# Loading the edge rows as 96 partitions and a rest, and making the first norm in two parts, in a graph network kernel

## The chip, the cores and the metric

The kernel runs on one core of one Trainium2 chip. The metric is the device time of one execution in microseconds (us, lower is better), as the median of three runs. The engines are named as in the profile: PE (TensorE, with PEld for its weight loads), DVE (VectorE), ACT (ScalarE), POOL (GpSimd) and SP (SyncE, which here only issues DMAs); PEq, ACTq and SPq are their instruction queues.

## The reference, cut to what matters

Four graph layers run one after the other on 6250 nodes of 128 features and 206250 edges sorted by destination. Each begins with a layer norm and a ReLU and adds its result to `x`. Only the first is touched here:

```python
h = relu(layernorm(x))                                        # the first norm
h_all = einsum('nd,rdf->nrf', h, weight)                      # 8 relations
gate_all = einsum('nd,rdo->nro', h, gate_weight)[..., 0]
msg = h_all[src, rel_type] * norm * sigmoid(gate_all[src, rel_type])[:, None]
out = relu(segment_sum(msg, dst, num_segments=6250))
```

## The kernel before

The nodes are padded to 6272, which is 49 tiles (`NT`) of 128 partitions. Before the edges of the first layer are walked, a setup block does two things side by side. All line numbers are those of the kernel before.

**The table.** The block makes `h`, the normed and rectified `x`, in 7 pieces (`PIECES`) of 7 tiles, and then a table in HBM (`table0`) that holds `sigmoid(gate) * h @ weight` for each node and relation, 512 KB for a tile of nodes. For tile t the work goes around four engines. PE turns `h[:, t, :]` over (L548), ACT copies the result out of PSUM (L492), PE multiplies it by the gate weights (L552) and by the eight relation weights (L558, called P(t) in what follows), ACT makes the sigmoid (L499), DVE scales four relations (L694, `gates`) and ACT the other four (L507), and SP stores the tile (L434, `store`). The staging buffer `out` has three places, so `gates(t)` and the ACT half of it wait until the store of tile t-3 has landed. P(t) waits for `gates(t-2)`, since PSUM has two places.

**The index work.** Beside it DVE checks whether the edges are sorted, finds the span of each chunk of 512 edges, and makes keys for pairs of nodes. It reads `dst_rows` (101 partitions, one for each round of 2048 edges) and `later` (the same list shifted by 256 edges). SP writes `rows_t` to HBM in four DMAs of 832 KB (L427), and POOL gathers from this table and from another (L649, L655).

The order on each engine's queue is written out by hand. SP issues its DMAs in program order, and the stores of the table stand behind L413, L417, L419, L422 and the four of L427:

```python
sp.dma_start(dst_rows, ...)                    # L413: 101 partitions
sp.dma_start(later[0:full, :], ...)            # L417: full = 100 partitions
sp.dma_start(later[full:full + 1, ...], ...)   # L419
sp.dma_start(next_first[0:ROUNDS - 1, :], ...) # L422: 100 elements
sp.wait_ge(s_rows_t, 7)
for k in range(MPT): sp.dma_start(flat_table[...], rows_t[...])  # L427, 4 times
store(0, 11)
```

On DVE the norm (`norm_vector`, L137) runs through the whole of `x` in each step before the next: the mean over all 49 tiles, seven subtractions, seven sums of squares, one variance, and after ACT's square root the seven scalings. Only behind the fifth and the seventh of these do the first `gates` come. ACT (`norm_scalar`, L165) alternates Square and ReLU over the pieces, then does one Sqrt, and only then begins with the tiles. Between calls of `gates`, DVE's index work is spread over tiles 4 to 45 (L709 to L839). PE has some of it too: `last_rows` (L571) after tiles 12 and 16, and `flip` (L584) after every second tile from 23 on.

The block ends with a barrier, and the loop over edges begins after it.

Of the kernel before, what the change touches and what calls it, by code (L numbers as in the profile page):

```python
# [18 lines left out]
NB = 4  # L19
ROUNDS = -(-E // (CH * NB))  # L20
# [9 lines left out]
EPS = 1e-5  # L30
# [22 lines left out]
PIECES = 7  # L53
PT = NT // PIECES
# [4 lines left out]
LIMIT = 256  # L59


def bass_gnn(nc, A):

    root = ExitStack()
    with root:
# [68 lines left out]
        def piece(k):  # L134
            return slice(k * PT, (k + 1) * PT)
# [131 lines left out]
        FLIPS = -(-PCOLS // 2)  # L267
        s_marks_in = root.enter_context(nc.semaphore("pair_marks_in"))
# [29 lines left out]
        with ExitStack() as l0:  # L298
# [17 lines left out]
            with ExitStack() as st:  # L316
# [81 lines left out]
                def _(sp):  # L398
# [3 lines left out]
                    for k in range(MPT):  # L402
# [10 lines left out]
                    sp.dma_start(dst_rows, A["dst_rows"].rearrange("(p k) e -> p (k e)", k=NB)).then_inc(s_rows, 16)  # L413
# [3 lines left out]
                    sp.dma_start(later[0:full, :], flat_dst[LIMIT:LIMIT + full * span]  # L417
                                 .rearrange("(p e) -> p e", e=span)).then_inc(s_later, 16)
# [17 lines left out]
                    store(0, 11)  # L436
                    sp.wait_ge(s_mark_t, 1)
                    sp.dma_start(flat_pairs[0:PSPAN].rearrange("(k p) -> k p", p=P), mark_t[:, :]).then_inc(s_mark_out, 16)
                    store(11, 13)
# [7 lines left out]
                    store(13, 20)  # L447
# [3 lines left out]
                    store(20, 22)  # L451
# [5 lines left out]
                    store(22, 38)  # L457
                    sp.wait_ge(s_gout, 2)
                    sp.dma_start(A["groups"].rearrange("(r a) b -> r a b", a=2), gout[:, :, :]).then_inc(s_g_out, 16)
                    store(38, 40)  # L460
# [3 lines left out]
                    store(40, NT)  # L464
# [5 lines left out]
                @block.scalar  # L470
                def _(act):
                    act.dma_start(rel, A["rel_cols"]).then_inc(s_rel, 16)
                    act.dma_start(x[:, :, :], A["x"].rearrange("(t p) d -> p t d", p=P)).then_inc(s_x, 16)
                    act.dma_start(w0[:, :].rearrange("p (r d) -> p r d", r=R), A["w0"].rearrange("r k d -> k r d")).then_inc(s_w, 16)
                    with nc.allow_non_contiguous_dma(reason="1024 gate weights, once"):
                        act.dma_start(g0[:, :], A["g0"].rearrange("r k a -> k (r a)")).then_inc(s_w, 16)
                    act.dma_start(weight0[:, :], A["weight_cols"]).then_inc(s_w, 16)
                    for b in range(0, BLOCKS, 2):
                        n = min(2, BLOCKS - b)
                        act.wait_ge(s_turned, 2 * (b + n))  # L480
                        nc.scalar.activation(rows_t[:, b:b + n, :, :].rearrange("p b e w -> p b w e"),
                                             pS[:, b // 2 % 2, 0:n * 2 * P].rearrange("p (b w e) -> p b w e", b=n, w=2),
                                             ACT.Copy).then_inc(s_rows_t, 1)
# [38 lines left out]
                    step(11, 22)  # L522
                    for m in range(FLIPS):
                        step(22 + 2 * m, 24 + 2 * m)
                        flip(m)
                    step(22 + 2 * FLIPS, NT + 2)
                    act.wait_ge(s_key, FLIPS)
                    act.wait_ge(s_x, 16)
                    act.wait_ge(s_w, 48)

                @block.tensor
                def _(pe):
# [55 lines left out]
                    step(0, 8)  # L588
# [3 lines left out]
                    step(8, 11)  # L592
                    pe.wait_ge(s_mark, 1)
                    nc.tensor.transpose(pS[0:PCOLS, 0, 0:P], mark[:, :], ident[:, :]).then_inc(s_mark_turned, 1)
                    step(11, 13)
# [5 lines left out]
                    step(13, 17)  # L601
# [3 lines left out]
                    step(17, 22)  # L605
                    for m in range(FLIPS):
                        step(22 + 2 * m, 24 + 2 * m)
                        flip(m)
                    step(22 + 2 * FLIPS, NT + 1)

# [50 lines left out]
                def _(dve):  # L661
# [36 lines left out]
                    def behind_norm(k):  # L698
                        if k == 4:
                            gates(0, 1)  # L700
                        if k == 6:
                            gates(1, 4)
                    dve.wait_ge(s_x, 16)
                    norm_vector(dve, norm0, h, between=behind_norm)

                    dve.wait_ge(s_rows, 16)
# [3 lines left out]
                    gates(4, 5)  # L710
                    dve.wait_ge(s_fall, 1)
                    nc.vector.tensor_reduce(fall[0:ROUNDS, 0:1], falls, AXX, ALU.max).then_inc(s_fall, 1)
                    gates(5, 7)
# [7 lines left out]
                    gates(7, 9)  # L721
                    dve.wait_ge(s_below, 2)
                    nc.vector.tensor_reduce(in_round[:, :], behind, AXX, ALU.add).then_inc(s_below, 1)
                    gates(9, 10)
# [19 lines left out]
                    gates(10, 12)  # L744

                    dve.wait_ge(s_later, 32)
                    nc.vector.memset(over[:, :], 0.0).then_inc(s_repeat, 1)
                    nc.vector.tensor_tensor(repeats, dst_rows, later, ALU.is_ge).then_inc(s_repeat, 1)
                    gates(12, 14)
                    dve.wait_ge(s_repeat, 2)  # L750
                    nc.vector.tensor_reduce(over[0:ROUNDS, :], repeats, AXX, ALU.max).then_inc(s_repeat, 1)
                    gates(14, 15)
# [6 lines left out]
                    cover(0)  # L759
                    cover(1)  # L760
                    gates(15, 16)
                    nc.vector.tensor_reduce(low[:, :, 0], by_chunk, AXX, ALU.min).then_inc(s_low, 1)
                    gates(16, 18)
                    cover(2)
                    cover(3)
                    gates(18, 19)
# [4 lines left out]
                    gates(19, 21)  # L771
# [16 lines left out]
                    gates(21, 23)  # L788
# [5 lines left out]
                    gates(23, 25)  # L794
                    keys(1)
                    gates(25, 27)
# [5 lines left out]
                    gates(27, 29)  # L802
                    keys(2)
                    gates(29, 31)
# [3 lines left out]
                    gates(31, 33)  # L808
                    keys(3)
                    gates(33, 35)  # L810
# [23 lines left out]
                    gates(35, 37)  # L834
                    keys(4)
                    gates(37, 41)
                    keys(5)
                    gates(41, 45)
                    keys(6)  # L839
                    gates(45, NT)  # L840
# [1347 lines left out]
```

## Time and profile before

| | |
|---|---|
| median of three runs | 6237.64 us (6236.5 to 6240.86) |
| the profiled execution | 6241.27 us, span 6239.5 us |
| setup block in the span | 0 to about 191 us |
| busy PE / DVE / ACT / POOL | 75% / 42% / 24% / 50% |
| DMA | 817.56 MB, mean 131 GB/s |

The setup block is some 3% of the span. It can be read from a timeline alone, since each instruction of it runs once or 49 times; the pages' averages over the whole span say little about it.

### The profile page before, as it was taken

The numbers are of one execution on the slowest core, as the hardware profiler recorded it, in microseconds if no ns is written. First come the engines' busy times: TensorE is split into PE (matmuls) and PEld (weight loads), VectorE is DVE, ScalarE is ACT, GpSimd is POOL, SyncE is SP. The second block draws the span as 40 slices with busy tenths as digits, with TensorE's granted clock in tenths as the row PEclk, the third lists the DMA queues.
The fourth block names the chain that finished last, engine by engine and source line by source line (L and its number), as shares of the span: only waits on it lengthen the run. The fifth ranks groups of instructions, "written<-read, shape, count | busy, mean of one in ns | idle before, by whom it ended". The sixth has DMA issues, their size and how long they took to land. (4 is left out here: it accounts for less than half of the span.)

```text
span 6239.5 us, 90775 instructions
## 1 busy us (share of the span) xinstructions
PE 4667.4 (75%) x25783; PEld 3126.0 (50%) x25784; DVE 2634.3 (42%) x6089; ACT 1472.9 (24%) x2786; POOL 3137.0 (50%) x3319
## 2 busy tenths in 40 slices
PE   5555555555555548888888888888899799999998
PEld 3444444444444435555555555555444444444444
DVE  6666666666666554444444444444312300000000
ACT  4211111111111123333333333333211211111000
POOL 3577777777777727777777777776000000000000
PEclk9555555555555568888888888888799899999999
DMA  6333333322333324444344434443345365555554
GB/s 218 110 94 94 94 94 94 92 87 84 93 94 94 105 80 125 132 133 133 125 131 133 133 123 133 133 133 96 136 159 162 99 200 191 187 193 190 192 193 150
DMA packets 337345, 817.56 MB, mean 131 GB/s; under 512 B 126590, under 2 KB 147633, under 8 KB 321059
## 3 DMA queue, kind: packets, MB, share of 16 engines
q1 hardware_dynamic: 217996, 516.64, 24.6%
q0 software_dynamic: 105568, 215.74, 12.7%
q10 hardware_dynamic: 13696, 84.07, 3.6%
q8 instruction: 51, 0.84, 0.1%
q14 instruction: 34, 0.28, 0.0%
HBM read 701.15 MB, written 114.23 MB: 131 GB/s over the span
## 5 line engine op out<-in xcount | busy, mean ns | idle before, releaser
L1388 POOL DMA_INDIRECT parts<-scratch_table,parts x1616 | 1541.2, 954 | 588.0 <-issue 480.1
L970 POOL DMA_INDIRECT parts<-scratch_table,parts x1616 | 1527.7, 945 | 554.5 <-issue 491.9
L185 PE MATMUL e_win<-parts 128*128 128x64 f32 x3232 | 783.0, 424 | 987.5 <-DMA parts<-scratch_table,parts 980.4
L185 PEld LDWEIGHTS e_win<-parts 128*128 128x128 f32 x3232 | 720.2, 328 | 1058.0 <-issue 1027.7
L1759 PE MATMUL c_sums<-ring,parts 128*128 128x512 bf16 (+1 forms) x3822 | 790.4, 368 | 21.0 <-ACT parts L2055 17.7
L1496 DVE TENSOR_TENSOR parts<-e_p,parts 128x512 f32<-128x512 f32 x404 | 279.4, 691 | 1160.5 <-PE e_p L1439 961.7
L185 PEld LDWEIGHTS e_win<-e_onehot,e_msg 128*128 128x128 f32 x3232 | 476.2, 211 | 245.3 <-issue 214.8
L1759 PEld LDWEIGHTS c_sums<-ring,parts 128*128 128x128 bf16 x3822 | 361.7, 98 | 430.1 <-issue 27.0
L1419 PE MATMUL e_p<-h,we 64*128 64x512 f32 x808 | 282.8, 772 | 365.7 <-DMA h<-in_edge_T 361.6
L222 DVE TENSOR_SCALAR parts<-e_iota,dst_rel,weight 128x64 f32<-128x64 f32 x1616 | 443.0, 335 | 254.8 <-issue 254.2
L1426 PE MATMUL e_p<-parts,we 128*128 128x512 f32 x808 | 518.0, 728 | 3.2 <-DVE parts L1503 2.9
L1439 PE MATMUL e_p<-wn1b,parts 128*128 128x128 f32 x3232 | 499.0, 301 | 0.0
L2116 DVE SCALAR_TENSOR_TENSOR c_y<-c_pO,dinv,c_bias 128x128 f32<-128x128 f32 x147 | 41.6, 344 | 1060.1 <-PE c_pO L2009 1060.1
L870 DVE TENSOR_TENSOR parts<-e_iota,key_both 128x1024 bf16<-128x1024 f32 x392 | 475.1, 1212 | 0.0
L1452 ACT ACTIVATE e_msg<-parts 128x512 f32<-128x512 f32 x404 | 254.5, 630 | 906.0 <-DVE parts L1496 901.8
L185 PE MATMUL e_win<-e_onehot,e_msg 128*128 128x64 f32 x3232 | 445.5, 286 | 4.5 <-DVE acc L234 4.4
L1439 PEld LDWEIGHTS e_p<-wn1b,parts 128*128 128x128 f32 x3232 | 418.9, 202 | 26.0 <-issue 1.0
L1460 ACT ACTIVATE e_tw<-h,cols 128x512 f32<-128x512 f32 x404 | 324.2, 803 | 348.9 <-DMA h<-in_time_rows 344.2
L1759 PE MATMUL p3S<-ring,parts 128*128 128x512 bf16 (+1 forms) x1911 | 392.2, 368 | 17.6 <-DMA ring<-scratch_counts 17.6
L1055 ACT ACTIVATE h<-e_banks 128x392 f32 x400 | 177.3, 494 | 848.6 <-PE e_banks L902 813.6
L872 DVE TENSOR_TENSOR square<-e_iota,key_both 128x784 bf16<-128x784 f32 x392 | 377.0, 962 | 0.0
L1759 PE MATMUL c_sums<-ring,h 128*128 128x512 bf16 (+1 forms) x1274 | 359.4, 368 | 3.3 <-issue 3.3
(259 smaller groups left out, 4614.7 us busy)
## 6 DMA issues: line engine op xcount, KB each, us to landing
ring<-scratch_counts SPq DMA_DIRECT2D x336, 896.0 KB, 4.7
h<-in_time_rows SPq DMA_DIRECT2D x101, 1024.0 KB
parts<-scratch_table,parts POOLq DMA_INDIRECT x3232
h<-in_edge_T SPq DMA_DIRECT2D x101, 512.0 KB, 3.9
scratch_counts<-h ACTq DMA_DIRECT2D x12, 3136.0 KB
scratch_counts<-type_mem ACTq DMA_DIRECT2D x12, 3136.0 KB
scratch_table<-type_mem SPq DMA_DIRECT2D x33, 512.0 KB, 2.7
scratch_table<-parts SPq DMA_DIRECT2D x16, 512.0 KB
```

Of the source, the lines that this page charges most:

```text
L185: last = nc.tensor.matmul(win[:, 0:W], rows[:, j, :], onehot[:, j, :], start=(j == 0), stop=(j == J - 1))
L222: last = nc.vector.tensor_scalar(onehot[:, j, :], columns, dst_rel[:, bass.ds(c * J + j, 1)], weight[:, bass.ds(c * J + j, 1)], ALU.is_equ ...
L870: nc.vector.tensor_tensor(u["lo_hot"][:, half, :, :], u["iota"][:, 0:P].unsqueeze(1).to_broadcast([P, PPC, P]), key_both[:, 0, bass.ds(at, ...
L872: nc.vector.tensor_tensor(u["hi_hot"][:, half, :, :], u["iota"][:, P:P + PW].unsqueeze(1).to_broadcast([P, PPC, PW]), key_both[:, 1, bass. ...
L970: pool.indirect_dma_start(rows[:, half * NB + b, j, :], None, A["table0"], bass.IndirectOffsetOnAxis(ap=staged[:, half, b * J + j:b * J + ...
L1388: pool.indirect_dma_start(rows[:, half * NB + b, j, :], None, A["table1"], bass.IndirectOffsetOnAxis(ap=staged[:, half, b * J + j:b * J + ...
L1419: nc.tensor.matmul(p1[:, k, :], we1[half, :], edge_in[half, at, b % NB // 2, :], start=True, stop=True).then_inc(s["p1"], 1)
L1426: nc.tensor.matmul(p2[:, b % 2, :], we2[:, :], hid[:, (b - P2) % NB, :], start=True, stop=True).then_inc(s["p2"], 1)
L1439: last = nc.tensor.matmul(p3[:, b % 2, j * P:(j + 1) * P], ef[:, k, j * P:(j + 1) * P], wn1b[:, :], start=True, stop=True)
L1460: nc.scalar.activation(tw[:, b % NB, :], time_in[:, at, b % NB, :], ACT.Sigmoid, bias=cols1[:, 3:4], scale=cols1[:, 2:3]).then_inc(s["tw"], 1)
L1496: nc.vector.tensor_tensor(z[:, k, :], p3[:, (b - 1) % 2, :], rows[:, slot, :, :].rearrange("p j d -> p (j d)"), ALU.add).then_inc(s["z"], 1)
L1759: last = nc.tensor.matmul(to, parts[part][:, bass.ds(t, 1), :], counts, start=(start and part == 0), stop=(stop and part == 2))
```

## The change

The 101 rows of `dst_rows` load as 96 partitions and 5, and the 100 of `later` as 96 and 4. The first norm is made in two parts: two pieces (14 tiles) go all the way through square root and scaling first, and the other five pieces follow in steps between the `gates` of tiles 0 to 13, with a second Sqrt on ACT between tiles 9 and 10. The mean's factor and the ReLU move into DVE's instructions (`scalar_tensor_tensor`), so that ACT does no ReLU. The index work, which before lay between tiles 4 and 45, now lies between tiles 14 and 41.

```diff
+EVEN = ROUNDS // 16 * 16
+        FLIP_AT = (27, 30, 31, 32, 33, 34, 35, 36, 37, 38, 39, 41, 42, 44)
+        halves = (slice(0, 2 * PT), slice(2 * PT, NT))
-  sp.dma_start(dst_rows, A["dst_rows"].rearrange("(p k) e -> p (k e)", k=NB)).then_inc(s_rows, 16)
+  for part in (slice(0, EVEN), slice(EVEN, ROUNDS)):
+      sp.dma_start(dst_rows[part, :], by_round[part, :]).then_inc(s_rows, 16)
-  sp.dma_start(later[0:full, :], ...).then_inc(s_later, 16)
+  for part in (slice(0, EVEN), slice(EVEN, full)):
+      sp.dma_start(later[part, :], by_later[part, :]).then_inc(s_later, 16)
...
@@ scalar
-  norm_scalar(act, norm0, h)
+  def squares(k):
+      act.wait_ge(norm0["centered"], k + 1)
+      if k >= 2:
+          act.wait_ge(norm0["reduced"], k - 1)
+      nc.scalar.activation(square[:, k % 2, :, :], h[:, piece(k), :], ACT.Square).then_inc(norm0["squared"], 1)
+  def root(i):
+      act.wait_ge(norm0["var"], i + 1)
+      nc.scalar.activation(std[:, halves[i]], var[:, halves[i]], ACT.Sqrt).then_inc(norm0["std"], 1)
-  step(0, 11)
+  squares(0); squares(1); root(0)
+  step(0, 2); squares(2); step(2, 3); squares(3); step(3, 4); squares(4)
+  step(4, 6); squares(5); step(6, 8); squares(6); step(8, 10); root(1); step(10, 21)
...
@@ tensor
-  step(0, 8)    # fall's sum   step(8, 11)   # mark   step(11, 13)  # last_rows(0, 1)
-  step(13, 17)  # last_rows(2, 3)   step(17, 22)   then flip(m) after step(22 + 2 * m, 24 + 2 * m)
+  step(0, 18)   # fall's sum   step(18, 21)  # mark   step(21, 23)  # last_rows(0, 1)
+  step(23, 27)  # last_rows(2, 3)                  then flip(m) after step(FLIP_AT[m], FLIP_AT[m + 1])
...
@@ vector
-  norm_vector(dve, norm0, h, between=behind_norm)
+  def center(k):
+      nc.vector.tensor_reduce(mean[:, piece(k)], x[:, piece(k), :], AXX, ALU.add)
+      nc.vector.scalar_tensor_tensor(h[:, piece(k), :], mean[:, piece(k)]..., -1.0 / D, x[:, piece(k), :], ALU.mult, ALU.add)
+  def scale(first, end):
+      for k in range(first, end):
+          nc.vector.scalar_tensor_tensor(h[:, piece(k), :], h[:, piece(k), :], 0.0, rstd[:, piece(k)]..., ALU.max, ALU.mult)
+  center(0); center(1); reduce(0, 2); variance(0, 2); factor(0); scale(0, 2); center(2)
+  gates(0, 1); center(3); gates(1, 2); reduce(2, 3); center(4); gates(2, 4); reduce(3, 4); center(5)
+  gates(4, 5); reduce(4, 5); gates(5, 6); center(6); gates(6, 7); reduce(5, 6); gates(7, 8); reduce(6, 7)
+  variance(1, PIECES); gates(8, 10); factor(1); scale(2, 3); gates(10, 11); scale(3, 5)
+  gates(11, 12); scale(5, 7); gates(12, 14)
   falls                # before: behind gates(1, 4)
+  gates(14, 15); fall; gates(15, 17); ... behind; gates(17, 18); in_round; gates(18, 20); mark ... window
+  gates(20, 22); repeats; gates(22, 23); over; gates(23, 24); low; gates(24, 25); high
+  gates(25, 26); cover(0); cover(1); gates(26, 27); keys(0); gates(27, 28); cover(2); cover(3)
+  gates(28, 29); keys(1); gates(29, 30); rest_lo; gates(30, 31); keys(2); gates(31, 32); dst_rel
+  gates(32, 33); keys(3); gates(33, 34); idx8; gates(34, 36); keys(4); gates(36, 38); groups
+  gates(38, 39); keys(5); gates(39, 41); keys(6); gates(41, NT)
```

SP's other small DMAs of the block keep their order among themselves and stand behind later stores than before (the marks behind tile 21 instead of 10, the spans behind 26 instead of 19).

## Rows read from the trace of the kernel before

**Rows 1.** Busy time of each engine by stretch, then PEclk, DMA share, GB/s.

```profile
18.00:24.00 6.00, 1.94 (x8) 1.57 (x8) 5.97 (x3) 1.15 (x1) 0.00 (x0) 1.00 1.17 265
...
36.00:42.00 6.00, 0.00 (x0) 0.00 (x0) 5.91 (x7) 1.72 (x3) 4.98 (x4) 1.00 0.60 156
50.00:66.00 16.00, 12.25 (x33) 6.26 (x34) 9.64 (x11) 8.17 (x26) 12.65 (x12) 1.00 0.16 50
66.00:80.00 14.00, 2.05 (x7) 0.95 (x7) 0.23 (x1) 0.40 (x3) 0.24 (x1) 0.67 0.98 299
81.00:182.50 101.50, 98.48 (x365) 50.08 (x365) 68.95 (x123) 67.19 (x277) 26.81 (x25) 0.98 0.66 249
```

**Rows 2.** Timeline of SP's queue: start and duration of issuing, in us.

```profile
25.55 0.25 SPq L413 DMA_DIRECT2D type_mem<-in_dst_rows  x1
25.85 9.85 SPq L417 DMA_DIRECT2D type_mem<-in_dst_rows  x1
...
36.05 6.95 SPq L422 DMA_DIRECT2D next_first<-in_dst_rows  x1
43.04 28.97 SPq L427 DMA_DIRECT2D scratch_counts<-parts  x4
72.13 3.33 SPq L434 DMA_DIRECT2D scratch_table<-type_mem  x2
```

**Rows 3.** The four DMAs of L427, issuing time in ns (min/median/max).

```profile
L427 SPq DMA_DIRECT2D scratch_counts<-parts x4: 2630/3372/19465, 43.0 to 69.2; - x4
```

**Rows 4.** Who waited for whom in 20 to 183 us.

```profile
PE pT L548 <- DVE h L160: 24.1, 1, 24.1
...
DVE type_mem L694 <- DMA scratch_table<-type_mem: 15.7, 2, 15.3
```

**Rows 5.** The table's stores (L434), from issue to landing.

```profile
DMA to landing us min/median/max: 2.6/2.7/7.6
```

**Rows 6.** Timeline of the norm and the first tiles on DVE, ACT and PE.

```profile
25.79 6.68 DVE L139 TENSOR_REDUCE mean<-x 128x49 f32<-128x6272 f32 x1
28.04 1.98 ACT L481 ACTIVATE parts<-pS 128x512 int16<-128x512 f32 x3 [0.35 <-PE pS L540]
32.73 7.10 DVE L144 TENSOR_TENSOR h<-x,mean 128x896 f32<-128x896 f32 x7
33.85 1.95 ACT L171 ACTIVATE square<-h 128x896 f32<-128x896 f32 x2 [3.83 <-DVE h L144]
48.62 1.09 DVE L149 TENSOR_REDUCE ssq<-square 128x7 f32<-128x896 f32 x1 [0.59 <-ACT square L171]
49.74 0.19 DVE L151 TENSOR_SCALAR var<-ssq 128x49 f32<-128x49 f32 x1
50.28 1.28 ACT L176 ACT_TABLE_LOAD   x1
51.58 0.25 ACT L176 ACTIVATE std<-var 128x49 f32<-128x49 f32 x1
54.41 0.59 PE L552 MATMUL pT<-g,acc 128*128 128x8 f32 x2 [0.15 <-ACT acc L492]
54.59 1.28 ACT L499 ACT_TABLE_LOAD   x1
```

**Rows 7.** Timeline of P(0), P(5), P(11), P(26) and P(48) on PE.

```profile
54.86 3.76 PE L558 MATMUL pW<-acc 128*128 128x512 f32 x4
...
81.14 3.57 PE L558 MATMUL pW<-acc 128*128 128x512 f32 x4 [13.09 <-ACT type_mem L507]
...
98.10 1.96 PE L558 MATMUL pW<-acc 128*128 128x512 f32 x4
...
132.53 1.96 PE L558 MATMUL pW<-acc 128*128 128x512 f32 x4
...
180.56 1.96 PE L558 MATMUL pW<-acc 128*128 128x512 f32 x4
```

**Rows 8.** DVE's groups from 80 to 182.7 us: busy us, mean ns, idle before.

```profile
L694 DVE TENSOR_TENSOR type_mem<-pW,acc 128x512 f32<-128x512 f32 x31 | 21.4, 689 | 35.9 <-PE pW L558 20.1 <-DMA scratch_table<-type_mem 15.7
...
L748 DVE TENSOR_TENSOR type_mem<-type_mem 101x2048 f32<-101x2048 int32 x1 | 2.3, 2286 | 0.0
```

More of the change, by code:

```diff
@@ L412, in _ @@
                                  far_marks[:, :].bitcast(F32)).then_inc(s_marks_out, 16)
-                    sp.dma_start(dst_rows, A["dst_rows"].rearrange("(p k) e -> p (k e)", k=NB)).then_inc(s_rows, 16)
+                    by_round = A["dst_rows"].rearrange("(p k) e -> p (k e)", k=NB)
+                    for part in (slice(0, EVEN), slice(EVEN, ROUNDS)):
+                        sp.dma_start(dst_rows[part, :], by_round[part, :]).then_inc(s_rows, 16)
                     flat_dst = A["dst_rows"].rearrange("c e -> (c e)")
@@ L416, in _ @@
                     full = (E - LIMIT) // span
-                    sp.dma_start(later[0:full, :], flat_dst[LIMIT:LIMIT + full * span]
-                                 .rearrange("(p e) -> p e", e=span)).then_inc(s_later, 16)
+                    by_later = flat_dst[LIMIT:LIMIT + full * span].rearrange("(p e) -> p e", e=span)
+                    for part in (slice(0, EVEN), slice(EVEN, full)):
+                        sp.dma_start(later[part, :], by_later[part, :]).then_inc(s_later, 16)
                     sp.dma_start(later[full:full + 1, 0:E - LIMIT - full * span],
@@ L435, in store @@
                                          out[t % 3].rearrange("p r d -> p (r d)")).then_inc(s_store[t % 3], 16)
-                    store(0, 11)
+                    store(0, 22)
                     sp.wait_ge(s_mark_t, 1)
                     sp.dma_start(flat_pairs[0:PSPAN].rearrange("(k p) -> k p", p=P), mark_t[:, :]).then_inc(s_mark_out, 16)
-                    store(11, 13)
+                    store(22, 24)
                     sp.wait_ge(s_mark_out, 16)
@@ L446, in _ @@
                                      .rearrange("(r k) -> r k", k=per)[:, 0:1]).then_inc(s_mark_in, 16)
-                    store(13, 20)
+                    store(24, 27)
                     sp.wait_ge(s_span, 1)
@@ L450, in _ @@
                                  low[:, :, :].rearrange("r b k -> r (b k)")).then_inc(s_meta_out, 16)
-                    store(20, 22)
+                    store(27, 29)
                     sp.wait_ge(s_meta_out, 16)
@@ L456, in _ @@
                     sp.dma_start(both, A["meta"].unsqueeze(0).to_broadcast([P, NC, 2])).then_inc(s_base_in, 16)
-                    store(22, 38)
+                    store(29, 40)
                     sp.wait_ge(s_gout, 2)
                     sp.dma_start(A["groups"].rearrange("(r a) b -> r a b", a=2), gout[:, :, :]).then_inc(s_g_out, 16)
-                    store(38, 40)
+                    store(40, 42)
                     sp.wait_ge(s_g_out, 16)
@@ L463, in _ @@
                                  .unsqueeze(0)).then_inc(s_g_in, 16)
-                    store(40, NT)
+                    store(42, NT)
                     sp.wait_ge(s_g_in, 16)
@@ L518, in flip @@
                             ACT.Copy).then_inc(s_key, 1)
-                    step(0, 11)
+                    squares(0)
+                    squares(1)
+                    root(0)
+                    step(0, 2)
+                    squares(2)
+                    step(2, 3)
+                    squares(3)
+                    step(3, 4)
+                    squares(4)
+                    step(4, 6)
+                    squares(5)
+                    step(6, 8)
+                    squares(6)
+                    step(8, 10)
+                    root(1)
+                    step(10, 21)
                     act.wait_ge(s_mark_turned, 1)
                     nc.scalar.activation(mark_t[:, :], pS[0:PCOLS, 0, 0:P], ACT.Copy).then_inc(s_mark_t, 1)
-                    step(11, 22)
+                    step(21, 27)
                     for m in range(FLIPS):
-                        step(22 + 2 * m, 24 + 2 * m)
+                        step(FLIP_AT[m], FLIP_AT[m + 1])
                         flip(m)
-                    step(22 + 2 * FLIPS, NT + 2)
+                    step(FLIP_AT[FLIPS], NT + 2)
                     act.wait_ge(s_key, FLIPS)
@@ L604, in _ @@
                         last_rows(n)
-                    step(17, 22)
                     for m in range(FLIPS):
-                        step(22 + 2 * m, 24 + 2 * m)
+                        step(FLIP_AT[m], FLIP_AT[m + 1])
                         flip(m)
-                    step(22 + 2 * FLIPS, NT + 1)
+                    step(FLIP_AT[FLIPS], NT + 1)
                 @block.gpsimd
@@ L696, in gates @@
                                 gate[:, t % 2, 0:R // 2].unsqueeze(2).to_broadcast([P, R // 2, D]), ALU.mult).then_inc(s_out, 1)
[L698 to L702, printed above, removed]
-                    dve.wait_ge(s_x, 16)
-                    norm_vector(dve, norm0, h, between=behind_norm)
-                    dve.wait_ge(s_rows, 16)
+                    def center(k):
+                        nc.vector.tensor_reduce(mean[:, piece(k)], x[:, piece(k), :], AXX, ALU.add).then_inc(norm0["summed"], 1)
+                        dve.wait_ge(norm0["summed"], k + 1)
+                        nc.vector.scalar_tensor_tensor(h[:, piece(k), :], mean[:, piece(k)].unsqueeze(2).to_broadcast([P, PT, D]),
+                                                       -1.0 / D, x[:, piece(k), :], ALU.mult, ALU.add).then_inc(norm0["centered"], 1)
@@ new lines, in reduce, with variance @@
+                    def reduce(first, end):
+                        for k in range(first, end):
+                            dve.wait_ge(norm0["squared"], k + 1)
+                            nc.vector.tensor_reduce(ssq[:, piece(k)], square[:, k % 2, :, :], AXX, ALU.add).then_inc(norm0["reduced"], 1)
+                    def variance(i, reduced):
+                        dve.wait_ge(norm0["reduced"], reduced)
+                        nc.vector.tensor_scalar(var[:, halves[i]], ssq[:, halves[i]], 1.0 / D, EPS, ALU.mult, ALU.add).then_inc(norm0["var"], 1)
@@ new lines, in factor @@
+                    def factor(i):
+                        dve.wait_ge(norm0["std"], i + 1)
+                        nc.vector.reciprocal(rstd[:, halves[i]], std[:, halves[i]]).then_inc(norm0["rstd"], 1)
+                        dve.wait_ge(norm0["rstd"], i + 1)
+                    def scale(first, end):
+                        for k in range(first, end):
+                            nc.vector.scalar_tensor_tensor(h[:, piece(k), :], h[:, piece(k), :], 0.0,
+                                                           rstd[:, piece(k)].unsqueeze(2).to_broadcast([P, PT, D]),
+                                                           ALU.max, ALU.mult).then_inc(norm0["h"], 1)
@@ new lines, in _ @@
+                    dve.wait_ge(s_x, 16)
+                    center(0)
+                    center(1)
+                    reduce(0, 2)
+                    variance(0, 2)
+                    factor(0)
+                    scale(0, 2)
+                    center(2)
+                    gates(0, 1)
+                    center(3)
+                    gates(1, 2)
+                    reduce(2, 3)
+                    center(4)
+                    gates(2, 4)
+                    reduce(3, 4)
+                    center(5)
@@ new lines, in _ @@
+                    gates(4, 5)
+                    reduce(4, 5)
+                    gates(5, 6)
+                    center(6)
+                    gates(6, 7)
+                    reduce(5, 6)
+                    gates(7, 8)
+                    reduce(6, 7)
+                    variance(1, PIECES)
+                    gates(8, 10)
+                    factor(1)
+                    scale(2, 3)
+                    gates(10, 11)
+                    scale(3, 5)
+                    gates(11, 12)
@@ L707, in _ @@
+                    scale(5, 7)
+                    gates(12, 14)
+                    dve.wait_ge(s_rows, 32)
                     dve.wait_ge(s_turned, 2 * BLOCKS)
@@ L709, in _ @@
                     nc.vector.tensor_tensor(falls, dst_rows[:, 0:NB * CH - 1], dst_rows[:, 1:NB * CH], ALU.is_gt).then_inc(s_fall, 1)
-                    gates(4, 5)
+                    gates(14, 15)
                     dve.wait_ge(s_fall, 1)
                     nc.vector.tensor_reduce(fall[0:ROUNDS, 0:1], falls, AXX, ALU.max).then_inc(s_fall, 1)
-                    gates(5, 7)
+                    gates(15, 17)
                     dve.wait_ge(s_next, 16)
@@ L720, in _ @@
                     nc.vector.tensor_tensor(behind, marks, pairs(MPR), ALU.is_lt).then_inc(s_below, 1)
-                    gates(7, 9)
+                    gates(17, 18)
                     dve.wait_ge(s_below, 2)
                     nc.vector.tensor_reduce(in_round[:, :], behind, AXX, ALU.add).then_inc(s_below, 1)
-                    gates(9, 10)
+                    gates(18, 20)
                     dve.wait_ge(s_below, 3)
@@ L743, in _ @@
                                                    ALU.mult, ALU.add).then_inc(s_window, 1)
-                    gates(10, 12)
-                    dve.wait_ge(s_later, 32)
+                    gates(20, 22)
+                    dve.wait_ge(s_later, 48)
                     nc.vector.memset(over[:, :], 0.0).then_inc(s_repeat, 1)
                     nc.vector.tensor_tensor(repeats, dst_rows, later, ALU.is_ge).then_inc(s_repeat, 1)
-                    gates(12, 14)
+                    gates(22, 23)
                     dve.wait_ge(s_repeat, 2)
                     nc.vector.tensor_reduce(over[0:ROUNDS, :], repeats, AXX, ALU.max).then_inc(s_repeat, 1)
-                    gates(14, 15)
+                    gates(23, 24)
                     def cover(n):
@@ L758, in cover @@
                                                 rest_dst[:, n * BANK + 1:end + 1], ALU.is_ge).then_inc(s_cover, 1)
-                    cover(0)
-                    cover(1)
-                    gates(15, 16)
                     nc.vector.tensor_reduce(low[:, :, 0], by_chunk, AXX, ALU.min).then_inc(s_low, 1)
[L763 to L766, printed above, removed]
+                    gates(24, 25)
                     nc.vector.tensor_reduce(high[:, :], by_chunk, AXX, ALU.max).then_inc(s_high, 1)
@@ L770, in _ @@
                     nc.vector.tensor_tensor(low[:, :, 1], high[:, :], low[:, :, 0], ALU.subtract).then_inc(s_span, 1)
-                    gates(19, 21)
+                    gates(25, 26)
+                    cover(0)
+                    cover(1)
+                    gates(26, 27)
                     def keys(i):
@@ L787, in _ @@
                     keys(0)
-                    gates(21, 23)
+                    gates(27, 28)
+                    cover(2)
+                    cover(3)
+                    gates(28, 29)
+                    keys(1)
+                    gates(29, 30)
                     dve.wait_ge(s_cover, 4)
@@ L793, in _ @@
                     nc.vector.tensor_scalar(rest_lo[:, 0:1], a_low[:, 0:1], unsorted[:, 0:1], None, ALU.mult).then_inc(s_ready, 1)
-                    gates(23, 25)
-                    keys(1)
-                    gates(25, 27)
+                    gates(30, 31)
+                    keys(2)
+                    gates(31, 32)
                     dve.wait_ge(s_base_in, 16)
@@ L801, in _ @@
                                             ALU.subtract).then_inc(s_ready, 1)
-                    gates(27, 29)
-                    keys(2)
-                    gates(29, 31)
+                    gates(32, 33)
+                    keys(3)
+                    gates(33, 34)
                     dve.wait_ge(s_rel, 16)
@@ L807, in _ @@
                                                    ALU.mult, ALU.add).then_inc(s_ready, 1)
-                    gates(31, 33)
-                    keys(3)
-                    gates(33, 35)
+                    gates(34, 36)
+                    keys(4)
+                    gates(36, 38)
                     per = PPG * GPR
@@ L833, in _ @@
                     nc.vector.tensor_scalar(gout[:, 0, :], tiles_of[:, 0, :], unsorted[0:GROUNDS, 0:1], None, ALU.mult).then_inc(s_gout, 1)
-                    gates(35, 37)
-                    keys(4)
-                    gates(37, 41)
+                    gates(38, 39)
                     keys(5)
-                    gates(41, 45)
+                    gates(39, 41)
                     keys(6)
-                    gates(45, NT)
+                    gates(41, NT)
                     dve.wait_ge(s_ready, 4)
```

4 lines of the change are left out of this document (2 added, 2 removed).

## The prediction, made before the changed kernel was run

> **What bounds the kernel now.** The change touches only the setup block, so I read that block by stretches, then SP's queue, the waits, and the timelines of the norm and the tiles. The last product of the block, P(48), starts at 180.56 [rows 7]; whatever moves it moves the barrier and all that follows, since nothing later is edited. From 81 us on PE is busy for 98.48 of 101.50 us, while DVE has 68.95 and ACT 67.19 [rows 1], so PE sets the pace there, one tile in about 2.05 us.
>
> What lies ahead of 81 us is not PE's. It waits 24.1 us for the first scaled piece of `h` [rows 4], and P(0) starts at 54.86 [rows 7]. Then comes a second hole: DVE stands 15.3 us for the store of tile 0 to land [rows 4], and P(5), which needs `gates(3)`, starts only at 81.14 [rows 7]. The store is late because SP issues it at 72.13, behind 28.97 us of L427, 6.95 of L422 and 9.85 of L417 [rows 2]. Of the four DMAs of L427 one took 19.465 us to issue and the least 2.63 [rows 3], so most of this is waiting, not issuing.
>
> Waiting for what is seen in the DMA share. With 128-partition loads in flight (18 to 24 us) it is about 1 at 265 GB/s; from 36 to 42, when the 100 rows of `later` move, it is 0.60 at 156 GB/s, about ten of sixteen engines; from 50 to 66 it is 0.16 at 50 GB/s, and POOL's 25 gathers of 32 KB are part of that; then, from 66 to 80, 0.98 at 299 GB/s as if a lid were lifted [rows 1]. I read: the 101 rows go through one engine, the 808 KB take until about 66 us there, that engine's queue is full, and every later DMA of SP that needs it waits. The cover over everything until 80 us is this one load.
>
> **The change, part by part.** *The split loads.* 96 partitions can be dealt evenly to sixteen engines, as 128 are. At the 265 GB/s of full share [rows 1], 1.6 MB take 6 us from 25.6. The two additional DMAs cost SP some 0.3 us each, by L413's 0.25 [rows 2], hidden since SP then waits for `rows_t` until 30.02 (ACT's copies end there [rows 6]). L427 without the blocking costs 2.63 to 3.4 us each [rows 3], 10.5 to 13.5 us: SP is free at 41 to 44 instead of 72. Its 3.4 MB need 11 to 12 us at 299 GB/s [rows 1], so the first stores, issued near 43, land by about 47.
> For the five and four rows left over no row of this trace has a price; it lies between nothing and 2 us (40 KB against the 808 KB of the slow load, which took 40 us), and nothing waits for them before tile 13. The Trainium skill, "DMA: Bandwidth & Descriptors", section "Why a DMA increments its semaphore by 16 and not by 1", says the number of engines is the largest up to 16 that divides the slowest dimension; by it the five rows use five engines, which leaves the sum as it is.
>
> *The norm's first part.* DVE begins at 25.79 as before. Two pieces: 0.95 for a mean (6.68 / 7), 1.01 for a subtraction (7.10 / 7) [rows 6], twice, ends near 30.0 with the semaphore waits. I cost the new fused instructions by the plain ones: same elements, same type. They could be 1.8 times dearer at most, by 1.0 against 1.83 us for two passes over 1616 elements; that would add 0.8 a piece and I keep it for the range. ACT is free at 30.02 and squares both in 1.95, to 32.0; the second sum (1.09) ends at 33.1, variance 0.19, square root 0.25, reciprocal some 0.3, first scaling 1.0: 35.1. P(0) comes 1.3 later, as from 53.59 to 54.86: **36.5** in place of 54.86.
> The Sqrt needs a table load of 1.28. In rows 6 the load for the sigmoid starts at 54.59, before the gate product that the sigmoid waits for has ended (54.41 + 0.59), so a load runs ahead of the wait; here it hides in 32.0 to 33.3. Were it behind the wait, P(0) is at 37.8.
>
> *P(0) to P(11).* P(2) comes 6.9 us after P(0), the first products being slow (3.76 against 1.96 [rows 7]), as before: 43.4. Nine tiles at 2.05 are 18.45. To this I add waits, found by walking DVE (`center` 2.05, `reduce` 1.09, `gates` 0.69 each) and ACT (Square 0.95, four scalings 1.15) in their new order. ACT takes `squares(4)` ahead of its half of tile 2, but `center(4)` ends only near 47.2: P(4) is 2.2 late. The same with `squares(5)` and `squares(6)`: 1.0 and 0.65. `root(1)` between tiles 9 and 10 brings two table loads that weren't there (Sqrt, then Sigmoid again), 2.6 us and the root: P(10) is 1.95 late. P(11) at 36.5 + 6.9 + 18.45 + 5.8 = **67.6**, where it was 98.10. Square behind Sigmoid needs no load of its own: in the GRU block 13 sigmoids and 13 squares alternate, and no load stands at a square.
> The Trainium skill, "ScalarE: Activation LUTs", section "What ACT_TABLE_LOAD costs", speaks against this part: each switch of set costs 2.66 us, a drain included. Rows 6 show 1.28 and the activation 0.02 later, no drain. By the page two more switches would cost 5.3 and not 2.6, and the time would be 2.8 us longer.
>
> *P(11) to P(26).* Before: 132.53 - 98.10 = 34.4 [rows 7], with all four `last_rows` in it. Now the `mark` turn falls into it (+1.2, from waiting for DVE), and two flips leave it (-0.5). DVE's index work, 38 us by 68.95 less 45 `gates` of 0.69 [rows 1, 8], had tiles 4 to 45 and now has 14 to 41. Passes of 2.3 us [rows 8] follow tiles 21, 22, 23 and 24, each with a `gates`: 2.9 us per tile against PE's 2.05. DVE is 3 us behind at `gates(25)`, and PE's `last_rows(2)` waits for `cover(0)` right behind it: +3.8. Further +1.0 for small waits. P(26) at 67.6 + 39.9 = **107.5**.
>
> *P(26) to P(48).* Before 48.0 [rows 7]. Two flips more (+0.5), and keys at every second tile put DVE at 20 us for eight tiles against PE's 18: the slack of one tile takes most, +0.6. P(48) at **156.6**.
>
> Sum: 180.56 - 156.6 = 24.0 us. I take 1 us off since stores at this pace meet POOL's gathers (before, two tiles waited 2.3 us for a landing in all, by rows 4 and its like; median landing 2.7, worst 7.6 [rows 5]). Gain 23. The profiled execution (6241.27) would go to 6218.3; it lies 3.6 above the median, so against the median **6215 us**.
>
> **The rivals.** *Part of it lost* (gain 8 to 17, 6221 to 6230): either L427 still issues slowly, because its 3.4 MB in small packets queue behind the rows, and `gates(3)` comes at 57 instead of 50 (-7); or DVE's dense stretch, with fused instructions at 1.8 times, delays `center` and `covers` by 5 to 8. For it: DVE's slack in tiles 21 to 33 is negative as it is. Against: L427's least is 2.63.
> *The load doesn't set SP free* (no gain): if the lid is something else, such as the writes' own packets, the store stays at 72 and `gates(3)` at 79.8. From `gates(3)` to P(48) the new order takes 106.7 us (49.9 to 156.6), before 100.8: P(48) at 186.5, +6, 6244. The jump of the share from 0.16 to 0.98 speaks against it.
> *The other side, slower*: a partition slice is put on one engine whole. Then `later`'s 768 KB, which had ten engines, join the 768 of `dst_rows`; 40 us for 808 KB become about 75, SP is free near 105, and P(48) is at 107 + 107 = 214: 6271. It decides from a first store later than 85 us. Against it: `later[0:full]` is itself a slice, and had 0.60.
> *More*: fewer waits of ACT and DVE than walked; all of them 11 us, half of it gives 6209.
>
> **How the numbers follow.** Within 0.2% (12.5 us) a measurement of this kernel can hardly be told from no change. Chances: forecast (gain 17 to 28, 6209 to 6221) 0.71; part lost 0.16; SP not free 0.07; slower by one engine 0.02; more than 28 gained 0.04. A range of 6207 to 6229 holds a little over 0.8. Faster by over 0.2% is 0.71 + 0.04 + 0.10 of the partial cases, 0.85; same 0.06 + 0.06, 0.12; slower 0.03.
>
> **What would show it.** L417, L422 issue in under 1 us each; L427's longest under 4; first store issued before 46 and no wait of DVE for a landing above 3 us; DMA share near 1 from 30 to 43. P(0) near 36.5, P(11) near 67.6, P(26) near 107.5, P(48) near 156.6. Five table loads on ACT in the block. Wrong would be a first store after 60, or a P(48) beyond 168; and any change of the 6050 us behind the barrier, of which I assume none.

## The result, and the profile after

The changed kernel takes 6215.94 us (median of 7 runs, 6212.96 to 6218.97) against 6237.64 (6235.92 to 6240.86). The ratio is 0.9966, 95% interval 0.9955 to 0.9976: 21.7 us less. The profiled execution has a span of 6213.0 us.

SP's queue, in the timeline of the changed kernel (L418 and L424 are the split loads, L428 `next_first`, L433 the four DMAs of `rows_t`, L440 the stores):

```profile
25.50 1.09 SPq L418 DMA_DIRECT2D type_mem<-in_dst_rows  x2
26.64 0.68 SPq L424 DMA_DIRECT2D type_mem<-in_dst_rows  x2
27.36 0.53 SPq L425 DMA_DIRECT2D type_mem<-in_dst_rows  x1
27.93 0.41 SPq L428 DMA_DIRECT2D next_first<-in_dst_rows  x1
30.00 10.78 SPq L433 DMA_DIRECT2D scratch_counts<-parts  x4
41.68 3.80 SPq L440 DMA_DIRECT2D scratch_table<-type_mem  x2
```

Where L417 and L422 took 9.85 and 6.95 us and L427 28.97 [rows 2], they now take 0.7, 0.4 and 10.8. The first store is issued at 41.68 and not at 72.13. The stretches say the same, with the columns of [rows 1]:

```profile
26.00:30.00 4.00, 3.48 (x14) 2.17 (x13) 3.93 (x4) 3.40 (x6) 0.00 (x0) 1.00 0.97 240
30.00:43.00 13.00, 7.97 (x20) 4.18 (x21) 9.69 (x13) 7.58 (x16) 9.63 (x10) 1.00 1.08 298
50.00:66.00 16.00, 13.30 (x44) 6.39 (x43) 13.01 (x17) 13.21 (x43) 10.87 (x10) 1.00 0.62 226
```

The DMAs are full from 26 to 43 us, and the stretch from 50 to 66, where they moved 50 GB/s beside the one slow load [rows 1], now carries the table.

On PE (L588) P(0), P(26) and P(48), with PE's wait for `cover(0)` in front of `last_rows` (L601) ahead of P(26); and on ACT the second root (L499) between its two table loads:

```profile
36.14 3.76 PE L588 MATMUL pW<-acc 128*128 128x512 f32 x4
...
60.40 1.28 ACT L499 ACT_TABLE_LOAD   x1
61.69 0.23 ACT L499 ACTIVATE std<-var 128x35 f32<-128x35 f32 x1
61.83 0.26 ACT L507 ACTIVATE acc<-pT 128x128 f32<-128x128 f32 x1
62.11 1.28 ACT L514 ACT_TABLE_LOAD   x1
...
106.05 2.42 PE L601 MATMUL pS<-rest_dst,last_of 128*128 128x512 f32 x4 [4.03 <-DVE parts L837]
108.76 3.64 PE L588 MATMUL pW<-acc 128*128 128x512 f32 x4
...
161.14 1.96 PE L588 MATMUL pW<-acc 128*128 128x512 f32 x4
```

P(0) starts at 36.14, P(11) at 66.80, P(26) at 108.76 and P(48) at 161.14, where the last was at 180.56 [rows 7]. The block's end can be read from the first instruction of DVE in the block behind it, a memset of `acc`. It starts at 193.0 us in the kernel before and at 173.5 in the changed one, and this mark serves for all that follows. The other 7 us by which the two profiled spans differ come later: the difference is 19.4 us at this mark, 22.4 at the next memset of `acc` (2308.2 and 2285.7) and 26.4 at the last store (6220.7 and 6194.3), in code that is the same. The medians differ by 21.7.

### The profile page after: what moved, and what is told of

It is laid out like the page before. It is cut to its first block and busy times, and to the rows that moved or that the text cites. A ratio compares the mean times of both kernels' runs of the same rounds, so it can differ in the third digit from the quotient of the medians.

```text
span 6213.0 us, 90779 instructions
## 1 busy us (share of the span) xinstructions
PE 4667.2 (75%) x25783; PEld 3124.9 (50%) x25784; DVE 2635.2 (42%) x6096; ACT 1469.4 (24%) x2782; POOL 3128.6 (50%) x3319
## 3 DMA queue, kind: packets, MB, share of 16 engines
q0 software_dynamic: 105568, 215.74, 12.7%
## 5 line engine op out<-in xcount | busy, mean ns | idle before, releaser
L1135 ACT ACTIVATE h<-e_banks 128x392 f32 x400 | 177.4, 494 | 847.0 <-PE e_banks L982 826.3
```

## The experiments

Twelve kernels ran, in three groups. The ratio of each is to the kernel before on the same chip, as recorded, with its 95% interval; it is not exactly the quotient of the two medians.

**One part alone.** The first group took the two parts of the change apart and then put other numbers of partitions in the place of 96. The kernel before took 6244.07 us on its chip.

`e1_split_only`: the kernel before with

```diff
-sp.dma_start(dst_rows, by_round)             # and later[0:full, :] whole
+for part in (slice(0, 96), slice(96, ROUNDS)): sp.dma_start(dst_rows[part, :], by_round[part, :])
+for part in (slice(0, 96), slice(96, full)): sp.dma_start(later[part, :], by_later[part, :])
...
```

> The kernel before with the split loads alone. Theory (the one-engine load closes SP's queue, and the norm's order sets the start of the tiles): P(0) stays at 54.9, SP is free near 41, the store of tile 0 is issued near 61 when tile 0 is done and lands near 65, gates(3) near 66 in place of 79.8, P(5) near 68 in place of 81.1, and the slow product behind the hole (3.57 against 1.96) goes too: P(48) near 166, about 14.5 us less, 6223 us. Rival (the split does nothing for SP; the gain is that of the norm's order): no change, 6238 us.

6228.51 us, ratio 0.9976 (0.9965 to 0.9986); the block ends at 177.3, 15.7 us before 193.0 (14.5 were expected). P(0) is at 54.74 and P(5) at 67.61, and SP in its timeline:

```profile
30.00 11.40 SPq L431 DMA_DIRECT2D scratch_counts<-parts  x4
60.28 3.02 SPq L438 DMA_DIRECT2D scratch_table<-type_mem  x2
```

The first store goes out as soon as tile 0 is made. The hole before P(5) is gone, and with it the slow product behind it: 1.96 in place of 3.57.

`e2_norm_only`: the changed kernel with both loads whole.

```diff
-for part in (slice(0, EVEN), slice(EVEN, ROUNDS)): ...   # and the same for later
+sp.dma_start(dst_rows, by_round)
+sp.dma_start(later[0:full, :], by_later)
```

> The changed kernel with the loads as before (101 and 100 partitions). Theory: P(0) near 36, but the first store is issued at 72 and gates(3) comes at 79.8 as before; from there the new order takes 112.5 us to P(48) (48.65 to 161.14 in the changed kernel), so P(48) near 192, about 11.7 us later than before, 6249 us. Rival (the norm's order alone brings the gain, the split is a detail): P(48) near 161, 6216 us.

6255.07 us, ratio 1.0015 (1.0006 to 1.0025): slower. The block ends at 205.7, 12.7 us later than in the kernel before. P(0) comes at 36.14, and then in the waits

```profile
DVE type_mem L721 <- DMA scratch_table<-type_mem: 33.8, 1, 33.8
```

DVE stands 33.8 us for the landing of the first store, where it was 15.3 [rows 4]. Starting earlier only lengthens this wait; and the new order, which keeps five pieces of the norm behind `gates(3)`, then has more left to do: from P(5) to P(48) it takes 111.1 us, the old order 99.4. So the two parts are worth -15.7 and +12.7 alone, and -19.4 together: on top of the split, the norm's order brings 3.7 us. These 3.7 us come from one trace of each kernel; the measured ratios of the whole change and of the split alone, 0.9966 and 0.9976, have intervals that overlap.

`e3_prime_parts` and `e4_94_parts`: the changed kernel with

```diff
-EVEN = ROUNDS // 16 * 16
+EVEN = 97        # e3: 97 and 4 partitions, 97 and 3
+EVEN = 94        # e4: 94 and 7 partitions, 94 and 6
```

> The changed kernel with the loads cut after 97 partitions in place of 96 (97 and 4, 97 and 3). Theory (the number of engines is a divisor of the partitions; 97 is prime, so both large parts go through one engine, 1.55 MB where the kernel before had 0.81 there in 40 us): SP is free only near 100, gates(3) near 105, P(48) near 218, 6275 us. Rival (cutting a load in two is what helps, by smaller transfers): as the changed kernel, 6216 us.

> The changed kernel cut after 94 partitions (94 and 7, 94 and 6). Theory: 94 is 2 times 47, so two engines; each has 0.75 MB to move, about the 0.81 MB that the one engine had in the kernel before, so SP is free near 70 and P(48) near 190, 6247 us. Rival (an even number of partitions, or any cut, is enough): as the changed kernel, 6216 us.

With 97: 6275.49 us, ratio 1.0049 (1.0033 to 1.0065), P(48) at 215.9, block end 228.3. With 94: 6247.44 us, ratio 1.0004 (0.9993 to 1.0014), so no different from the kernel before, P(48) at 185.5, block end 197.9. The two loads of `later` and the four of `rows_t` in SP's queue with 97 partitions:

```profile
35.78 31.15 SPq L424 DMA_DIRECT2D type_mem<-in_dst_rows  x2
66.97 1.51 SPq L425 DMA_DIRECT2D type_mem<-in_dst_rows  x1
68.52 0.85 SPq L428 DMA_DIRECT2D next_first<-in_dst_rows  x1
69.42 27.05 SPq L433 DMA_DIRECT2D scratch_counts<-parts  x4
96.60 3.15 SPq L440 DMA_DIRECT2D scratch_table<-type_mem  x2
```

and with 94:

```profile
27.89 8.20 SPq L424 DMA_DIRECT2D type_mem<-in_dst_rows  x2
...
37.15 29.11 SPq L433 DMA_DIRECT2D scratch_counts<-parts  x4
66.39 3.64 SPq L440 DMA_DIRECT2D scratch_table<-type_mem  x2
```

The same bytes in the same number of DMAs leave SP free for its first store at 41.7 us with 96 partitions, 66.4 with 94 and 96.6 with 97. Cutting is not what helps, nor is an even number. The share of busy DMA engines with 97 partitions, first beside POOL's gathers and then with every other engine idle:

```profile
26.00:66.00 40.00, 17.57 (x54) 8.91 (x52) 17.71 (x20) 15.50 (x36) 25.11 (x25) 0.76 0.15 47
...
85.00:90.00 5.00, 0.00 (x0) 0.00 (x0) 0.00 (x0) 0.00 (x0) 0.00 (x0) 0.50 0.06 26
90.00:95.00 5.00, 0.00 (x0) 0.00 (x0) 0.00 (x0) 0.00 (x0) 0.00 (x0) 0.50 0.76 227
```

A share of 0.06 is one engine of sixteen, and it moves 26 GB/s. With 94 partitions the share from 50 to 60 us is 0.22, with 97 it is 0.16 there, beside the same nine gathers of POOL: one engine more. The three times so fit sixteen, two and one engines. The Trainium skill, "DMA: Bandwidth & Descriptors", section "Why a DMA increments its semaphore by 16 and not by 1", gives this rule: the largest number up to 16 that divides the slowest dimension on both sides of the copy. This case agrees with it at 96, 94 and 97 partitions.

**What ACT's table loads cost, and waits in the new order.** The chip of the second group was another one: the kernel before took 7262.41 us there, and all its kernels some 1000 more. On it DVE and ACT show long waits that the profile puts down to "remote", no engine or DMA of the program that it could find, between 49 and 68 and between 117 and 142 us. The ends of the block are therefore not compared with 173.5, and of these four kernels mainly stretches between such waits are read.

`e5_third_root`:

```diff
-step(10, 21)
+step(10, 13)
+nc.scalar.activation(high_std, var[:, 0:2 * PT], ACT.Sqrt)
+step(13, 21)
```

> The changed kernel with one more Sqrt on ACT, of numbers that nothing reads, between tiles 12 and 13, and so two more table loads. Theory (a switch costs the row's 1.28 us and no drain): 2 x 1.28 + 0.2 for the root are 2.8 us on ACT, of which ACT's slack of one tile takes some 0.5 to 1: P(13) or P(14) 2 us late, the block's end 1 to 2.5 us later than 173.5. Rival (each switch costs 2.66 us with a drain, as the Trainium skill has it in ScalarE: Activation LUTs, What ACT_TABLE_LOAD costs): a gap of 1.4 us behind each load in the timeline, 5.5 us on ACT, and the block's end 4 to 5 us later.

7255.03 us, ratio 0.9985 (0.9974 to 0.9995). ACT in its timeline:

```profile
82.25 1.28 ACT L551 ACT_TABLE_LOAD   x1
83.55 0.22 ACT L551 ACTIVATE high_std<-var 128x14 f32<-128x14 f32 x1
83.67 0.26 ACT L508 ACTIVATE acc<-pT 128x128 f32<-128x128 f32 x1
83.95 1.28 ACT L515 ACT_TABLE_LOAD   x1
85.24 0.18 ACT L515 ACTIVATE acc<-pT 128x8 f32<-128x8 f32 x1
```

The activation follows 0.01 or 0.02 us after its load, twice. P(13) starts 3.75 us after P(12) and not 2.05, and the 1.7 us are still there at P(25): 32.9 us after P(12), 31.2 in `e7_squares_later`, which has the same order there. So a pair of switches costs 2.6 us on ACT and 1.7 on the table. At the block's end nothing of it can be read: 200.6 us, where the other three kernels of this chip have 199.7 to 200.5. The Trainium skill ("ScalarE: Activation LUTs", section "What ACT_TABLE_LOAD costs") puts one switch at 2.66 us, drain included. That would show as a gap of 1.4 us behind the load, and there is none, so here the measurement decides.

`e6_last_rows_later`, `e7_squares_later`, and `e8_both` with the two edits:

```diff
 # e6, tensor
-step(23, 27); last_rows(2); last_rows(3)
+step(23, 28); last_rows(2); last_rows(3)
-step(FLIP_AT[m], FLIP_AT[m + 1]); flip(m)
+step(max(28, FLIP_AT[m]), FLIP_AT[m + 1]); flip(m)
 # e7, scalar
-step(3, 4); squares(4); step(4, 6); squares(5); step(6, 8)
+step(3, 5); squares(4); step(5, 7); squares(5); step(7, 8)
```

> The changed kernel with PE's last_rows(2) and (3) behind tile 27's product in place of tile 25's, and the first flip one step less far. Theory (PE stands 4.0 us there for DVE's cover(0), and its next product is slow, 3.6 against 2.0): both go, P(26) comes near 103, and the block ends 4 to 5.7 us earlier than 173.5. Rival (DVE is the bound in tiles 21 to 33 anyway, so that PE only waits elsewhere): under 1.5 us.

> The changed kernel with ACT's squares(4) and squares(5) one tile later each, so that ACT scales tiles 2 and 4 without waiting for center. Theory (P(4) and P(6) wait 1.7 and 1.8 us for ACT's half of the tiles before, which stands behind the squares): 2 to 3 us come back at P(8) and at the block's end, 170.5 to 171.5. Rival (DVE, with center, reduce and gates, is what sets tiles 3 to 9, and ACT's wait only follows it): under 1 us.

> Both edits of the two kernels before this one. Theory: they add up, 6.5 to 8.5 us, block end 165 to 167, some 6209 us where the changed kernel has 6216. Rival (what one gives, the other loses in DVE's backlog): no more than the larger of the two alone.

7247.30, 7244.31 and 7244.53 us, ratios 0.9976 (0.9964 to 0.9988), 0.9975 (0.9964 to 0.9986) and 0.9973 (0.9963 to 0.9983), which can't be told apart. P(4) starts at 47.34 with squares later (48.92 in the changed kernel). P(26) follows P(25) by 2.3 us with `last_rows` later and by 8.7 without. But P(29) starts at 141.5, 141.9 and 142.2 in the three, and 143.2 in `e5_third_root`, whatever came before: the long wait ends there.

The third group repeated two of these beside the changed kernel itself, with a fourth kernel that also moves PE's other waits:

```diff
 # e9: in addition
-FLIP_AT = (27, 30, 31, ...)     step(0, 18); fall's sum; step(18, 21); mark's turn; step(21, 23)
+FLIP_AT = (28, 31, 32, ...)     step(0, 20); fall's sum; step(20, 22); mark's turn; step(22, 23)
```

> The changed kernel once more, as the reference of this group, since the chip of the group before moved its DMAs more slowly (the kernel before took 7262 us there, and tiles 5 to 8 and 27 to 29 waited for stores to land). Where the DMAs run as in the first runs: block end 173.5, some 22 us under the kernel before. Where they are slow again: a block end near 200.

> last_rows(2) and (3) behind tile 27's product, again. On the slow chip P(26) already followed P(25) by 2.3 us in place of 8.7, but the store's landing took it back at P(28). Theory: with DMAs as in the first runs, 4 to 5.7 us of it reach the block's end against the changed kernel of this group. Rival (DVE's backlog gives it back): under 1.5 us.

> With squares(4) and (5) one tile later too, again. On the slow chip P(4) came 1.7 us earlier. Theory: 2 to 3 us more than last_rows alone at the block's end, 6.5 to 8.5 in all. Rival (DVE sets tiles 5 to 9): P(4) earlier, P(8) not.

> The kernel with both edits, and in addition PE's sum of fall two steps later, the turn of mark one step later, and all flips one step later. Theory (PE's remaining waits for DVE, 1.5 us at P(17), 1.3 at P(20) and 0.9 to 1.3 each at three flips, are of order, not of DVE's total work, since DVE is idle 27 of 98 us from 60 to 158): another 3 to 5 us, block end 9 to 13 us under the changed kernel. Rival (DVE's backlog between tiles 21 and 33 sets the pace through the two places of PSUM, whatever PE's own order): under 1.5 us more.

The kernel before took 7254.51 us here, so this chip was like the second.

| | us | ratio to before | P(25) | P(29) | P(48) | block end |
|---|---|---|---|---|---|---|
| changed | 7243.86 | 0.9986 (0.9977 to 0.9996) | 115.2 | 142.5 | 188.7 | 201.1 |
| last_rows later | 7240.43 | 0.9988 (0.9978 to 0.9998) | 113.9 | 142.4 | 187.4 | 199.8 |
| and squares later | 7244.27 | 0.9985 (0.9974 to 0.9996) | 114.4 | 141.8 | 187.6 | 200.0 |
| and sum, mark, flips later | 7242.27 | 0.9984 (0.9974 to 0.9993) | 110.3 | 139.1 | 183.9 | 196.2 |

From P(25) to P(27) the changed kernel takes 12.3 us, `last_rows` later 7.4: the 5 us are real there. At the block's end 1.2 are left of them, and squares later adds nothing. Only the last kernel is 4.8 us earlier at the end. All three stay below what was expected (4 to 5.7 us, 6.5 to 8.5, and 9 to 13). The rest ends in waits like these of the changed kernel on this chip (timeline, 126 to 144 us):

```profile
138.32 0.69 DVE L723 TENSOR_TENSOR type_mem<-pW,acc 128x512 f32<-128x512 f32 x1 [7.69 <-remote]
...
141.02 0.28 ACT L507 ACTIVATE acc<-pT 128x128 f32<-128x128 f32 x1 [12.06 <-remote]
```

The expectations took these waits for stores that land late; the profile names no store for them. What all eight traces of the two slower chips show is where they stand: beside POOL's two runs of 25 gathers. The last wait of each stretch ends 3.9 to 4.9 us after the last gather of its run starts (in the changed kernel the gathers at 61.8 and 136.5 us, the waits' ends at 65.9 and 141.0). In the last kernel that gather starts at 132.7 us, 3.8 sooner than in the changed one, so its 4.8 us may come by way of the gathers and not of PE's own waits. In the traces of the changed kernel and of the first group the same gathers run without such waits, and whether they are the cause isn't tested. Whether 5 to 9 us can be had on a chip without the waits isn't shown. No version that beats the changed kernel by a measured time came out of this; the change's own gain on this chip is 0.14%, not 0.34%.

## Why the prediction was right

**The lid.** Right in mechanism and size. SP was to be free at 41 to 44 and was at 40.8; the block of L433 was to take 10.5 to 13.5 us and took 10.8. `e3_prime_parts` and `e4_94_parts` show that it was the engines per load. `e3_prime_parts` takes the course that the rival "slower" described: 1.0049, with the first store at 96.6 and P(48) at 215.9, where the rival had SP's release near 105 and P(48) at 214.

**The norm's first part.** P(0) was foretold at 36.5 and came at 36.14. The fused instructions took 1.09 us a piece, near the plain 1.01 and far from 1.8 times that. The load of the root ran ahead of its wait: it ends at 32.90, the variance starts at 32.91, the root at 33.12.

```profile
31.62 1.28 ACT L499 ACT_TABLE_LOAD   x1
33.12 0.21 ACT L499 ACTIVATE std<-var 128x14 f32<-128x14 f32 x1 [0.21 <-DVE var L740]
```

**P(0) to P(11).** Foretold 31.1 us, measured 30.7. The three long waits are where the walk had put them, their sizes less so: 1.7 ahead of P(4) (foretold 2.2), 1.8 ahead of P(6) (1.0), 1.5 ahead of P(10) from the second root (1.95). P(8) lost 0.2 in place of 0.65, P(3) 0.8 where nothing was foretold, and the first two products took 0.7 less. That the sum is met to 0.4 us owes something to these cancelling.

**P(11) to P(26).** Foretold 39.9, measured 42.0. PE's wait for `cover(0)` was put at 3.8 and is 4.03. Two things were left out. `fall`'s sum moves into this stretch just as the turn of `mark` does: before, P(7) came 3.6 us after P(6) for it, now P(17) comes 3.6 us after P(16), 1.5 more than usual. And what stands between the wait and P(26) is slow: the `last_rows` pair takes 2.42 us where the first pair takes 1.88, and this place costs 1.1 us more, wait apart, than in the kernel before. For these 1.5 and 1.1 us the sum had only its 1.0 for small waits.

**P(26) to P(48).** This term was mis-sized: foretold 49.1, measured 52.4. I had let DVE's backlog of keys pass for 0.6 us because the two places of PSUM take up a tile of lag, but PE's `flip` waits for DVE in PE's own queue, where no slack helps: 0.5 us at the first, for `cover`, and 0.7 and 1.1 at two others, for `keys`. And the wait at `cover(0)` has a tail. Behind it the granted clock is 0.50, the lower of its two levels, in both stretches from 106 to 112 us, and the product takes 3.64 in place of 1.96:

```profile
106.00:109.00 3.00, 2.96 (x8) 1.92 (x9) 0.59 (x1) 0.28 (x2) 2.15 (x3) 0.50 0.16 44
109.00:112.00 3.00, 3.00 (x4) 1.14 (x5) 0.00 (x0) 1.18 (x5) 2.39 (x3) 0.50 0.33 82
112.00:120.00 8.00, 7.51 (x34) 3.94 (x33) 7.38 (x18) 4.93 (x20) 6.01 (x7) 0.99 0.69 243
```

The row for that price was at hand in P(5), 3.57 behind a hole [rows 7], and I used it only for the hole that goes.

So PE's wait for `cover(0)` cost 4.0 us as itself and some 2.8 more in slow work, 1.1 ahead of P(26) and 1.7 in P(26) itself, which the sum did not have. The block gave 19.4 us where 24.0 less 1 were foretold, and the whole 21.7. The last 2.3 us are within what the later, unchanged code varies by (7 us between the two traces above). That the 6215 was met to 1 us is thus partly luck: the block was overrated by 3.6 us.

**What the prediction didn't ask** is what each part is worth. Its sum starts from a P(0) that is 18.4 us earlier. In `e1_split_only` P(0) comes 18.6 us later than in the changed kernel, and P(48) only 3.7 later (164.87 and 161.14). Of the 14.9 us given back, 2.4 go before P(11), where the rest of the norm and the second root now lie, 7.5 between P(11) and P(26) and 4.9 behind it: index work that lay under 41 tiles lies under 27, and PE waits for it.

## What to carry to other kernels

When the DMA share of a stretch is a small steady fraction and a DMA takes microseconds to issue, look at the partitions of what was issued just before: one load on one engine blocks a whole queue, and 101, 97 or 94 partitions are far dearer than 96 and a rest. When two edits meet in one pipeline, work out each alone as well: here the second was a loss without the first and, by the traces, a fifth of the block's gain with it. Starting a pipeline earlier is worth only what the engines beside it can still hide, and a wait of PE can also cost slow products behind it: here behind 4.0 us (3.64 for the product in place of 1.96), but not behind the waits of 1.0 and 1.1 us in the same trace.

## What the runs showed of the hardware that I had not expected

- The chips of the three groups ran the same kernel before in 6244, 7262 and 7255 us. On the two slower ones DVE and ACT wait for "remote" (22.3 us of ACT at L507 and 16.5 of DVE at L723 in the setup block of the changed kernel, 648 of ACT at L1135 between 200 and 2200 us), on the first chip no wait is put down so. The DMA share from 30 to 43 us is the same (1.07 and 1.08, at 289 and 298 GB/s), so in that stretch the DMAs are hardly slower, though the expectation of `e10_changed_again` took them to be. What the engines wait for stays open; no run told it apart.
- A DMA behind a load on one engine is held at its issue until that load is nearly over, though it moves on all engines itself. With 97 partitions one of the four of `rows_t` took 18.49 us to issue, from 71.88 to 90.37. The DMA share is 0.06 from 85 to 90 us and 0.76 from 90 to 95, and 1.08 from 30 to 43 us in the changed kernel, where nothing holds `rows_t`.
